# Attention on one core: TensorE takes scores and products tile by tile, two tiles apart, in place of pairs of tiles

## What is computed

```
xn  = layernorm(x)
q   = split_heads(xn @ q_w.T + q_b) / sqrt(32)       # 16 heads of 32 channels
k   = split_heads(xn @ k_w.T + k_b)
v   = split_heads(xn @ v_w.T + v_b)
ctx = softmax(q @ k.T) @ v                           # per batch and head, 2048 x 2048 scores
out = x + (ctx @ out_w.T + out_b) + tanh(xn @ weight @ aux_weight1 @ aux_weight2 + ffn_bias)
```

## Time and profile before

| | |
|---|---|
| median of 3 runs | 4641.23 us (4627.87 to 4641.38) |
| profiled execution, its own time | 4647.09 us |
| its span, first to last instruction | 4645.3 us |
| mean granted clock of TensorE over the span | 0.983 |
| TensorE matmul busy | 4555.9 us, 98% |
| GpSimd busy | 3197.8 us, 69% |
| VectorE busy | 2937.3 us, 63% |
| ScalarE busy | 2460.2 us, 53% |
| attention heads | from about 825 us to 4460 us of the span |

### The profile page before, as it was taken

The page is one execution under the profiler, slowest core; times in us unless marked ns, Lnnn a source line. Parts: engine busy times, 40 slices in busy tenths (PEclk is TensorE's granted clock), DMA queues, the critical chain, the costliest instruction groups (busy, mean ns, idle before and its releaser), DMA issues.

```text
span 4645.3 us, 81083 instructions
## 1 busy us (share of the span) xinstructions
PE 4555.9 (98%) x23776; PEld 2481.1 (53%) x23776; DVE 2937.3 (63%) x4928; ACT 2460.2 (53%) x4517; POOL 3197.8 (69%) x863
## 2 busy tenths in 40 slices
PE   7999999999999999999999999999999999999999
PEld 5888888444444444444444444444444444444457
DVE  3434343777767776767676767777676767677524
ACT  1222221366666666666666666666666666666631
POOL 0222222588888888888888888888888888888830
PEclk9999999799999999999999999999999999999999
DMA  4444444211111111212211121111211222211157
GB/s 152 163 154 163 154 160 163 57 42 43 43 43 42 43 45 43 50 43 53 43 42 43 42 43 43 43 43 43 45 42 43 51 46 48 43 42 42 47 171 255
DMA packets 288290, 338.44 MB, mean 73 GB/s; under 512 B 169984, under 2 KB 171008, under 8 KB 275584
## 3 DMA queue, kind: packets, MB, share of 16 engines
q1 hardware_dynamic: 286384, 332.48, 26.3%
q10 hardware_dynamic: 1488, 0.79, 0.1%
HBM read 195.30 MB, written 137.36 MB: 72 GB/s over the span
## 4 chain that ended last, share of the span: by engine, by line
PE 76%; issue 3%; DVE 2%; ACT 1%; DMA 0%; ACTq 0%; DVEq 0%; SPq 0%
PE sm_bank L773 25%; PE st_bank L789 20%; PE pv_bank L795 20%; PE sum_bank L795 7%; PE sm_bank L190 3%; DVE part_max L714 2%; PE st_bank L190 1%; ACT probs L645 1%; PE sm_bank L782 0%; DMA q_stack<-max_row 0%; DVE k_stack L728 0%; DMA s_sums<-sum_copy 0%; DVE probs L736 0%; DMA sums_col<-s_sums 0%; ACT q_stack L663 0%
## 5 line engine op out<-in xcount | busy, mean ns | idle before, releaser
L714 DVE TENSOR_REDUCE part_max<-sm_bank 128x1 f32<-128x512 f32 x4096 | 2502.2, 682 | 904.4 <-PE sm_bank L773 903.8
L612 POOL TENSOR_TENSOR pool_sum<-pool_sum,probs 128x2048 f32<-128x2048 f32 x576 | 2637.0, 4578 | 474.1 <-ACT probs L645 451.0
L645 ACT ACTIVATE probs<-st_bank 128x512 f32<-128x512 f32 x4096 | 2183.0, 604 | 1102.3 <-PE st_bank L789 1065.2
L773 PE MATMUL sm_bank<-k_stack,q_stack 96*128 96x512 f32 x4096 | 1849.7, 455 | 38.7 <-issue 17.4
L789 PE MATMUL st_bank<-q_stack,k_stack 97*128 97x512 f32 x4096 | 1651.4, 404 | 15.2 <-ACT probs L645 11.0
L773 PEld LDWEIGHTS sm_bank<-k_stack,q_stack 96*128 96x128 f32 x4096 | 782.6, 191 | 990.9 <-DVE part_max L714 622.6
L795 PE MATMUL pv_bank<-probs,v_head 128*32 128x512 f32 x8192 | 1029.8, 603 | 0.0
L789 PEld LDWEIGHTS st_bank<-q_stack,k_stack 97*128 97x128 f32 x4096 | 783.4, 191 | 160.1 <-ACT probs L645 73.3
L795 PEld LDWEIGHTS pv_bank<-probs,v_head 128*32 128x32 f32 x8192 | 214.4, 109 | 494.1 <-issue 370.1
L612 POOL TENSOR_TENSOR pool_sum<-probs 128x2048 f32<-128x2048 f32 x64 | 293.4, 4585 | 143.5 <-ACT probs L645 143.5
L795 PE MATMUL sum_bank<-probs,ones_att 128*32 128x512 f32 x2560 | 338.1, 600 | 0.0
(11 more groups left out here) (84 smaller groups left out, 2034.7 us busy)
## 6 DMA issues: line engine op xcount, KB each, us to landing
q_stack<-s_q_hi SPq DMA_DIRECT2D x128, 256.0 KB, 4.6
k_stack<-s_k_hi SPq DMA_DIRECT2D x128, 256.0 KB, 6.1
x_in<-in_x SPq DMA_DIRECT2D x16, 1024.0 KB, 7.7
s_q_hi<-qk_hi SPq DMA_DIRECT2D x16, 1024.0 KB, 4.3
s_q_lo<-qk_lo SPq DMA_DIRECT2D x16, 1024.0 KB, 6.4
s_k_hi<-qk_hi SPq DMA_DIRECT2D x16, 1024.0 KB, 4.3
s_k_lo<-qk_lo SPq DMA_DIRECT2D x16, 1024.0 KB, 6.4
s_v<-v_out SPq DMA_DIRECT2D x16, 1024.0 KB, 4.3
```

The costliest lines, as they stand in the source:

```text
L612: nc.gpsimd.tensor_tensor(total[:], one[:], probs[kt % PROBS][:], ALU.add).then_inc(pool_added, 1)
L645: nc.scalar.activation(probs[kt % PROBS][:, q * BLK:(q + 1) * BLK], st_bank[:, st_place(kt * QB + q)], ACT.Exp, scale=SCALE).then_inc(prob ...
L714: nc.vector.tensor_reduce(part_max[:, k:k + 1], sm_bank[:, sm_place(sm_slot(k))], AX.X, ALU.max).then_inc(max_scores_read, 1)
L773: nc.tensor.matmul(sm_bank[:, sm_place(sm_slot(k))], q_st[r][0:ROWS, q * P:(q + 1) * P], k_st[r][0:ROWS, b * BLK:(b + 1) * BLK], start=Tru ...
```

## The change

TensorE's order becomes tile by tile: both_scores of tile kt, then `use` of tile kt - 2 (`LAG`). `add_partial` stays behind tile 3 of the following head. No other engine's program changes, and no matmul, wait or buffer is added or taken away.

```diff
+LAG = 2
...
-            for p in range(CUT // 2):
-                both_scores(0, 0, 2 * p, 1, 2)
-                both_scores(0, 0, 2 * p + 1, 1, 2)
-                if p:
-                    use(0, 0, 2 * p - 2)
-                    use(0, 0, 2 * p - 1)
+            for kt in range(CUT):
+                both_scores(0, 0, kt, 1, 2)
+                if kt >= LAG:
+                    use(0, 0, kt - LAG)
 
             def body(h, r, more, following):
                 r1 = (r + 1) % GROUP
-                for p in range(CUT // 2, KT // 2):
-                    both_scores(h, r, 2 * p, following, more)
-                    both_scores(h, r, 2 * p + 1, following, more)
-                    use(h, r, 2 * p - 2)
-                    use(h, r, 2 * p - 1)
-                if more >= 1:
-                    for p in range(CUT // 2):
-                        both_scores(following, r1, 2 * p, following + 1, more - 1)
-                        both_scores(following, r1, 2 * p + 1, following + 1, more - 1)
-                        if p == 0:
-                            use(h, r, KT - 2)
-                            use(h, r, KT - 1)
-                        else:
-                            use(following, r1, 2 * p - 2)
-                            use(following, r1, 2 * p - 1)
-                        if p == 1:
-                            add_partial(h, r)
-                else:
-                    use(h, r, KT - 2)
-                    use(h, r, KT - 1)
+                for kt in range(CUT, KT):
+                    both_scores(h, r, kt, following, more)
+                    use(h, r, kt - LAG)
+                for kt in range(CUT if more >= 1 else LAG):
+                    if more >= 1:
+                        both_scores(following, r1, kt, following + 1, more - 1)
+                    if kt < LAG:
+                        use(h, r, KT - LAG + kt)
+                    else:
+                        use(following, r1, kt - LAG)
+                    if kt == CUT - 1:
+                        add_partial(h, r)
```

## The result

The changed kernel takes 4683.9 us (median of 5, 4667.0 to 4688.2) where the one before takes 4639.6 us (median of 5): ratio 1.0097, 95% interval 1.0074 to 1.0119. It is slower by 44 us. The forecast was 4618 us and faster, its range 4590 to 4664: wrong in sign, and outside the range.

What follows compares the result with a forecast made beforehand. VectorE's maxima were taken to slow TensorE in one half of each pair and idle in the other. Heads 22, turns 4 and pairs without maxima 3 us, off 4647.1, gave 4618 us, range 4590 to 4664.

Steps and rivals of the forecast that it cites:

- The head: An ordinary head of 16 slots, six with a sum: 54.48 us against 54.83, 22 us off over 63 heads.
- slot: One new round, 8 score matmuls and one tile's products: 1.74 + 0.33 + 1.00 = 3.07 us, 0.86 more with a sum.
- the wait at unit 22: New wait at the skip in the ring of `st_bank`: 0.20 us once a head, bounds nothing and 0.42 us.
- The pairs without maxima: Ten pairs at the end, waiting for ScalarE: 5.53 us becomes 5.24 in two slots, 3 us off in all.
- What stays hidden: GpSimd's additions, `copy_pv`, `copy_sums` and the row of maxima to `q_stack` stay covered in each head, costed at nothing.
- the sum's 25 us: Gain of the order without turns: 22 us from ordinary heads and 3 us from pairs without maxima.
- the one on the turns: At each of 15 loop turns, 0.3 us less held time in TensorE's burst: 4 us off in all.
- The clock: Lower granted clock for 6.6 us behind a turn, costing 3.3 us; count kept at 9 of 15, none 29 us less.
- Rival 1: At the turns TensorE idles less and no stretch at the lower clock follows: 4589 us, faster; chance 13%.
- Rival 2: Switches between matmul kinds eat the gain, 0.015 to 0.02 us more a slot: 4635 us, same; chance 22%.
- Rival 3: From last score to first product TensorE waits for the record's end, 0.40 us for 0.33: 4689 us, slower; chance 17%.

Runs made afterwards that it cites:

- e8: The kernel before, with the programs of TensorE, ScalarE and VectorE for the 64 heads written out, so none turns: 4580.5 us, ratio 0.9873.
- e7: The change, with the programs of TensorE, ScalarE and VectorE for the 64 heads written out, so none turns: 4555.1 us, ratio 0.9822.
- e1: The change, with the old pair order for tiles 10 and 11 of every fourth head, where VectorE turns: 4614.3 us, ratio 0.9955.
- e4: The kernel before, with tile order for tiles 10 and 11 of every fourth head alone: 4673.2 us, ratio 1.0080.
- e3: The change, with the old pair order for tiles 2, 3, 10 and 11 of every fourth head: 4602.5 us, ratio 0.9924.
- e2: The change, with the old pair order for tiles 2 and 3 of every fourth head, ahead of TensorE's turn: 4689.8 us, ratio 1.0113.

## Why the prediction was wrong

*The head* was right: slot 3.07 (3.05 to 3.06 measured), with a sum 3.93 (3.92), head 54.48 (54.45). Two terms were slightly off and cancelled: the wait at unit 22 is 0.27, not 0.20 us (median slot of tile 5 3.33, its neighbour 3.06), and the 16 slots of 3.06 make up for it.

*The pairs without maxima* agree by luck (3 us put; the last head is 4.1 us shorter). In ScalarE's timeline of the last head three pairs with a sum go from 6.36 and 6.37 us to 6.21 to 6.25, some 0.15 us each, half of the 0.29 put; the one without a sum goes from 5.57 to 5.63. Between e8 and e7 a pair gains 0.12 to 0.17. Most of the 4.1 us are two pairs of 8.28 us that the last head has before: each holds a stretch of 3.4 us at the lower clock, and after there is none between these two copies of `pv_bank`.

*What stays hidden:* GpSimd's additions, the copies and the row of maxima cost nothing in these heads, as put. Without turns, e7 against e8, the sum's 25 us are measured as 25.4.

*The step that failed* is the one on the turns: "In slots the first two stay, 1.0 and 0.8 us, but nothing in the burst behind them is held a second time. I take 0.3 us off each". It costed the turns against a burst, and left VectorE's aside with "comes eight tiles later". VectorE's turn has a length, 3.0 us, and a cover, the products between two bursts; that cover went from 2.7 us to 1.0. The same question was asked of GpSimd, and the answer given with a number; of VectorE's turn it was not asked, though the earlier trace rows show 3.2 us a turn of which the two held places account for 1.8. At TensorE's own turn 0.3 us were to be saved; 0.8 us of queued work were lost, and 0.5 us of waits for ScalarE saved, so it is 0.3 us more.

Where the 64.5 us of the 14 heads come from: TensorE idles 23 us more for VectorE and 12 us more behind its own turn, and 7 us less for ScalarE; the order itself should have saved 5 us (14 times 0.37). That leaves some 42 us for the lower clock, whose 99 us of further stretches would cost 49 if all of that time were bound by TensorE. That split is worked out, not run by itself: in e1 the held time and the stretches go together. But e4, where the stretches hardly grow, shows the held time as a loss of its own.

*The clock.* Its cost was bounded as "all, 19 us more": it allowed one kind of stretch, of 6.6 us behind TensorE's turn, at 15 places. What came was a second place for it, with up to 10.2 us each time. The bound was taken from rows in which VectorE's turn was covered, so it was no bound for the change.

*The rivals.* Rival 1 (the clock comes free) is what e3 and e7 show in part, and in the change the contrary holds. Rival 2 lost by the slots themselves. Rival 3 has the sign and, at 4689 us, nearly the time, by luck: its mechanism, a switch that waits for the end of the last score's record, is not in the trace (0.32 us, not 0.40). The real one is a wait for VectorE at 14 turns with the lower clock behind it, and it was not among the rivals.

The Trainium skill's page "Runtime: NRT & Kernel Launch", section Instruction fetch mechanics, says that a taken branch out of the prefetched pages stalls the engine until its target is fetched, and that this is a reason to write loops out. It gives no figure; the traces agree, and give one: 2.8 to 3.5 us from VectorE's branch to its next instruction, and nothing of it in the written-out program. In the traces before and after, of e1 and of e4, an 8 KB transfer of the profile's kind "instruction" starts 1.0 to 1.5 us behind each of VectorE's 14 branches. And e7 is 129 us below the change.

## What to carry over

A loop's turn is a wait with a length, on each engine at its own place in the program. Before shortening a burst, look for the longest piece of work that its neighbours use as cover once in many rounds, not only for what they need in each round. Where an order pays in the steady state and loses at the turns, keep the old order at the turns alone (e3), or write the loop out (e7).

## What the runs showed of the hardware

- VectorE's turn took 2.8 to 3.5 us and ScalarE's 2.4 to 2.8 us from the branch to the next instruction; a round of their loops is 538 and 646 recorded instructions. GpSimd's and SyncE's loops, with 138 and 164, turned in 0.26 to 0.33 us. TensorE idled 0.95 to 1.54 us at its own turn with 2.7 us of work queued, and 1.69 to 2.48 us with 1.9 us queued.
- Bursts in which TensorE idled 2.3 us or more for VectorE's turn were followed by 3.4 to 10.2 us at the lower clock at 41 of 42 turns (the change, e2, e4); bursts in which it idled 0.5 to 1.0 us (before, e1, e3), by none. But behind TensorE's turn the stretches came and went (58, 37, 51, 27, 3 us in the traces of before, the change, e1, e3, e4) with no rule that these runs settle.
- Changing from 128-column to 32-column matmuls right behind an undisturbed burst takes 0.32 us from start to start (median) against 0.235 of pitch; behind the slowed bursts of before it takes 0.33.
